# A two-layer graph network on 12,500 nodes and 200,000 edges: the vector path's first part turned behind the second map, edge sources spread by DMA, three result tables in place of four, and h stored by SyncE

## The reference, cut to what matters

```python
# layer 1: attention
h = (x @ W).reshape(N, H, C)
e = leaky_relu(a_src[src] + a_dst[dst]); alpha = softmax of e over dst
out = elu(segment_sum(h[src] * alpha, dst) + bias + x @ skip_W)
x = layernorm(x + out)
# layer 2: equivariant
w = silu(silu(edge_attr @ fc_w1) @ fc_w2) @ fc_w3      # wA, wB, wC, wD per edge
es, ev = ys[dst], yv[dst]                              # mapped node features
m0a = wA * es * sh0
m0b = wD * einsum('eud,ed->eu', ev, sh1) * INV_SQRT3
m1a = wB[:, :, None] * es[:, :, None] * sh1[:, None, :]   # vector path, first part
m1b = wC[:, :, None] * ev * sh0[:, :, None]               # vector path, second part
ns = segment_sum(concat([m0a, m0b]), src)
nv = segment_sum(concat([m1a, m1b]), src)
os_ = ns * dn @ w2_s + sc_s;  ov = nv * dn mapped by w2_v + sc_v   # the second map
x = layernorm(x + normalised concat([os_, ov]))
```

## Time and profile before

| | |
|---|---|
| median of 3 runs | 7266.64 us (7259.7 to 7271.49) |
| profiled execution, its time | 7338.37 us |
| profiled execution, its span | 7335.8 us |
| granted clock of PE, mean | 0.96 |
| busy in the span | PE 88%, DVE 71%, POOL 65%, ACT 57% |
| DMA | 1244.70 MB, mean 170 GB/s |

### The profile page before, as it was taken

One profiled execution on the slowest core, in us unless ns is written; L12 is line 12 of the kernel. 1 busy time (PEld: TensorE's weight loads), 2 busy tenths in 40 slices (PEclk: granted clock), 3 DMA queues, 4 the chain that ended last, 5 costly groups with the idle time before them and its releaser, 6 DMA issues.

```text
span 7335.8 us, 210965 instructions
## 1 busy us (share of the span) xinstructions
PE 6443.9 (88%) x42774; PEld 4394.0 (60%) x42775; DVE 5231.9 (71%) x16784; ACT 4207.1 (57%) x11999; POOL 4802.6 (65%) x4057
## 2 busy tenths in 40 slices
PE   6778777777777777787999999999999999999976
PEld 5444444444444444454777777777777777777754
DVE  3666666667666666799777777777777777777779
ACT  2444444444444444444677777777777777777732
POOL 3555555555555555454677777777777777777778
PEclk8998999999999999888999999999999999999999
DMA  5677777777777777644788888888888888888899
GB/s 181 184 194 197 197 194 193 196 195 197 196 199 193 196 197 196 184 155 147 134 141 140 141 139 141 139 141 139 141 140 140 140 140 141 139 141 139 141 238 300
DMA packets 1213481, 1244.70 MB, mean 170 GB/s; under 512 B 216576, under 2 KB 1124737, under 8 KB 1213345
## 3 DMA queue, kind: packets, MB, share of 16 engines
q0 software_dynamic: 328176, 468.28, 39.5%
q1 hardware_dynamic: 885266, 776.00, 36.4%
HBM read 641.49 MB, written 602.17 MB: 170 GB/s over the span
## 4 chain that ended last, share of the span: by engine, by line
PE 54%; issue 18%; SPq 17%; POOL 4%; DVE 3%; another core or an unknown queue 2%; DMA 1%; ACT 1%; DVEq 1%; POOLq 0%; ACTq 0%
PE PS L929 12%; PE PS L957 12%; PE PS L939 10%; PE PS L976 8%; SPq L398 7%; PE PS L984 5%; SPq L409 2%; PE PS L852 2%; SPq L405 2%; SPq L401 2%; SPq L395 2%; PE PS L989 2%; POOL arena L558 1%; PE PS L842 1%
## 5 line engine op out<-in xcount | busy, mean ns | idle before, releaser
L577 POOL DMA_INDIRECT part<-arena,c_idx x1664 | 2658.4, 1598 | 911.2 <-issue 522.3
L538 POOL DMA_INDIRECT big<-h_tab,big x1664 | 1647.3, 990 | 1217.1 <-PE PS L852 598.0
L852 PE MATMUL PS<-big 128*128 128x260 f32 x3328 | 1092.2, 439 | 387.3 <-DVE big L1172 257.1
L1172 DVE TENSOR_TENSOR big<-big,PS 128x260 f32 x1664 | 701.8, 422 | 684.7 <-PE PS L852 429.8
L1310 DVE TENSOR_TENSOR arena<-PS,arena 128x384 f32<-128x384 f32 x832 | 463.9, 558 | 987.2 <-PE PS L976 958.3
L852 PEld LDWEIGHTS PS<-big 128*128 128x128 f32 x3328 | 580.6, 203 | 760.9 <-issue 653.7
L929 PEld LDWEIGHTS PS<-ident,arena 128*128 128x128 f32 x6656 | 714.4, 141 | 500.3 <-issue 497.7
L929 PE MATMUL PS<-ident,arena 128*128 128x128 f32 x6656 | 909.6, 280 | 2.0 <-DVE arena L1333 2.0
L957 PE MATMUL PS<-arena,w2m 128*64 128x128 f32 (+1 forms) x6656 | 903.3, 392 | 0.0
L722 ACT COPY arena<-PS 128x512 f32<-128x512 f32 x1664 | 894.2, 589 | 10.8 <-PE PS L929 10.4
L939 PE MATMUL PS<-arena 128*128 128x256 f32 x3328 | 856.5, 380 | 1.1 <-ACT arena L744 1.1
(11 more groups left out here) (182 smaller groups left out, 11029.3 us busy)
## 6 DMA issues: line engine op xcount, KB each, us to landing
w_tab<-big SPq DMA_DIRECT2D x416, 520.0 KB
arena<-w_tab SPq DMA_DIRECT2D x1664, 130.0 KB
part<-arena SPq DMA_DIRECT2D x1664, 32.1 KB
ot_tab<-big SPq DMA_DIRECT2D x416, 128.0 KB
arena<-ot_tab SPq DMA_DIRECT2D x416, 128.0 KB
arena<-part SPq DMA_DIRECT2D x392, 128.5 KB, 3.5
big<-h_tab,big POOLq DMA_INDIRECT x1664
part<-arena,c_idx POOLq DMA_INDIRECT x1664
```

Of the source, the lines that this page charges most:

```text
L538: pool.indirect_dma_start(hg[:, s, k, :], None, h_tab, bass.IndirectOffsetOnAxis(ap=sidx[:, s, k:k + 1], axis=0)).then_inc(s_hg[s], 16)
L577: pool.indirect_dma_start(part[q], bass.IndirectOffsetOnAxis(ap=c_idx[:, s, k:k + 1], axis=0), o_cmb[:, s, k, :], None, compute_op=ALU.add ...
L852: mm(PS[:, 2 + k % 2, 0:HW], oh[:, p, k, :], hg[:, p, k, :], start=True, stop=True).then_inc(s_agg, 1)
L1172: v.tensor_tensor(x, x, PS[:, 2 + k % 2, 0:HW], ALU.add).then_inc(s_acc, 1)
```

## The change

Five edits come together.

1. The vector path's first part is wB * es * sh1 for three directions, and the second map does not act on directions. The kernel after puts wB * es alone into `mid` (component 2), maps it once (A), and multiplies the mapped result by `sh1` behind the map (`turned`, DVE), adding the mapped second part (D0, D1, D2). So `mid` has 6 components in place of 8, and 3 transposes of 128 by 128 a tile in place of 4. The map is now S (all 128 rows of the array), A (rows 0 to 63), D0 and D1 together (rows 64 to 127) and D2 (rows 0 to 63), for each of 2 tiles. Five blocks of 128 by 128 are transposed back instead of four. ACT's last copy takes 128 columns (S) where it took 512, and ACT copies `sh1` aside (`c_sh`).
2. The sources of 4 tiles are spread to 128 partitions by one DMA (`same` itself is its target), and DVE compares in place; the load of `c_parts`, the matmul with ones and the bf16 parts in the setup go.
3. Three result tables (`TABLES_OUT`) in place of four: 3 zero stores a step in stage A, 3 loads and 3 matmuls a block in stage D. Add i waits for add i-3. POOL's loop is unrolled by 12.
4. The stores of h go from POOL's program to SP's, between the loads of x and of the weights.
5. On PE the y matmuls of stage C stand ahead of the sum and the count.

The diff, cut to its core:

```diff
-    src_tab = dram("src_tab", [T, 2, P], BF16)
+    src_tab = dram("src_tab", [T, P], F32)
...
-    part = [dram(f"part{k}", [NG * 32 * ZERO, OR], F32) for k in range(GROUP)]
+    part = [dram(f"part{k}", [NG * 32 * ZERO, OR], F32) for k in range(TABLES_OUT)]
...
-        mid = cut(2 * PAIR * 2 * D).rearrange("p (s k c u) -> p s k c u", s=2, k=PAIR, c=8)
-        midT = cut(PAIR * 4 * P).rearrange("p (k c e) -> p k c e", k=PAIR, c=4)
-        oT_sb = cut(4 * P).rearrange("p (j e) -> p j e", j=4)
...
+        mid = cut(2 * PAIR * 6 * MUL).rearrange("p (s k c u) -> p s k c u", s=2, k=PAIR, c=6)
+        midT = cut(PAIR * 3 * P).rearrange("p (k c e) -> p k c e", k=PAIR, c=3)
+        oT_sb = cut(5 * P).rearrange("p (j e) -> p j e", j=5)
...
-        Y_BANK, T_BANK, SR_BANK, OT_BANK, SUM_BANK, CNT_BANK = (0, 1), (2, 3), 4, 5, 6, 7
-        counts = PS[:, CNT_BANK, 0:PAIR * 2].rearrange("p (k c) -> p k c", k=PAIR)
+        c_sh = sb("c_sh", [P, TURN, PAIR, 3])
+        Y_BANK, T_BANK, O_BANK, OT_BANK, SUM_BANK = (0, 1), (2, 3), 4, (5, 6), 7
+        oT = PS[:, 5:7, :].rearrange("p b n -> p (b n)")[:, P:6 * P].rearrange("p (j e) -> p j e", j=5)
+        OT_S, OT_A, OT_D = 0, 1, (3, 2, 4)
+        o_s = PS[:, T_BANK[1], 3 * P:4 * P]
+        o_v = PS[:, O_BANK, :].rearrange("p (j k u) -> p k j u", j=4, k=PAIR)
...
+            load_x(2, 0, CHUNK)
+            store_h(0, 0)
...
+            load(w2m[0:MUL, 2, :], w2_v[MUL:2 * MUL, :])
             for i in range(2):
+                load_x(3 + i, 1 - i, (2 + i) * CHUNK)
+                store_h(1 + i, 1 - i)
...
-                    for k in range(GROUP):
+                    for k in range(TABLES_OUT):
                         sp.dma_start(part[k][ds(g * (32 * ZERO), 32 * ZERO), :].rearrange("(p r) d -> p (r d)", p=32),
                                      zeros[:, :]).then_inc(s_zero, 16)
                     wait(sp, s_wev, 6 * (g - 3))
...
-                if s % 2 == 0 and there(u + 2):
-                    q = (s + 2) % TURN
-                    wait(sp, s_csr, u)
-                    sp.dma_start(c_parts[:, q // 2, :].rearrange("w (k e) -> w k e", k=GROUP),
-                                 src_tab[ds((u + 2) * PAIR, GROUP), :, :].rearrange("k w e -> w k e")
-                                 ).then_inc(s_cpa[q], 16)
...
+                if s % 2 == 0 and there(u):
+                    wait(sp, s_csum, u - 2)
+                    wait(sp, s_ccnt, u - 2)
+                    sp.dma_start(same[:, s:s + 2, :, :].rearrange("p s k e -> p (s k e)"),
+                                 src_tab[ds(u * PAIR, GROUP), :].rearrange("(o k) e -> o (k e)", o=1
+                                                                          ).to_broadcast([P, GROUP * P])
+                                 ).then_inc(s_cpa[s // 2], 16)
...
-            def store_h(c, s):
-                wait_apart(pool, s_hev, 2 * CHUNK * (c + 1))
-                pool.dma_start(hv[ds(c, 1)].rearrange("o p k d -> (o p) k d"), h_out[:, s, :, :]
-                               ).then_inc(s_hst[s], 16)
...
                         wait_apart(pool, s_ccmb, u + 1)
-                        wait_apart(pool, s_add[q], 8 * u - 8 * (s % 2))
-                        pool.indirect_dma_start(part[q], bass.IndirectOffsetOnAxis(ap=c_idx[:, s, k:k + 1], axis=0),
+                        wait_apart(pool, s_add[other], 8 * u + 4 * (k + 4 - TABLES_OUT - other))
+                        pool.indirect_dma_start(part[(r * PAIR + k) % TABLES_OUT],
+                                                bass.IndirectOffsetOnAxis(ap=c_idx[:, s, k:k + 1], axis=0),
                                                 o_cmb[:, s, k, :], None, compute_op=ALU.add).then_inc(s_add[q], 16)
...
+                    a.copy(oT_sb[:, :, :], oT).then_inc(s_coTsb, 1)
...
-                    a.copy(o_sb[:, :, :].rearrange("p k (j u) -> p k j u", j=4),
-                           PS[:, T_BANK[0], :].rearrange("p (j k u) -> p k j u", j=4, k=PAIR)).then_inc(s_cosb, 1)
+                    a.copy(o_sb[:, :, 0:MUL], o_s.rearrange("p (k u) -> p k u", k=PAIR)).then_inc(s_cos, 1)
+                if there(u):
+                    wait(act, s_cw[s], landed(u, s, PAIR))
+                    wait(act, s_cov, u - 3)
+                    a.copy(c_sh[:, s, :, :], wt[:, s, :, D + 1:D + 4]).then_inc(s_csh, 1)
...
-                    for first, n_comps in ((0, 1), (1, 3)):
...
+                    for row, which, chunk, n_chunks, to in ((0, 0, 0, 1, OT_S), (0, 1, 1, 1, OT_A), (MUL, 1, 1, 2, OT_D[0]),
+                                                            (0, 2, 2, 1, OT_D[1])):
+                        rows_used = slice(row, P if which == 0 else row + MUL)
                         for k in range(PAIR):
-                            if first == 0:
+                            if which == 0:
                                 wait(pe, s_cmT, PAIR * (u - 1))
-                            last = mm(PS[k * MUL:(k + 1) * MUL, OT_BANK, first * P:(first + n_comps) * P],
-                                      w2m[:, min(first, 1), :],
-                                      midT[:, k, first:first + n_comps, :].rearrange("p c e -> p (c e)"),
-                                      start=True, stop=True, tile_position=(0, k * MUL))
+                            last = mm(oT[k * MUL:(k + 1) * MUL, to:to + n_chunks, :].rearrange("p j e -> p (j e)"),
+                                      w2m[rows_used, which, :],
+                                      midT[rows_used, k, chunk:chunk + n_chunks, :].rearrange("p c e -> p (c e)"),
+                                      start=True, stop=True, tile_position=(row, k * MUL))
                     last.then_inc(s_coT, 1)
                 if there(u + 1):
...
-                if there(u - 3):
-                    sum_equal()
-                    count()
...
+                    wait(pe, s_coTsb, u - 1 if there(u - 2) else u - 2)
...
                     wait(pe, s_coTsb, u - 1)
-                    wait(pe, s_cmT, PAIR * (u - 1) + 1 if there(u - 1) else PAIR * (u - 1))
-                    for j in range(4):
-                        last = nc.tensor.transpose(PS[:, T_BANK[0], j * P:(j + 1) * P], oT_sb[:, j, :], ident[:, :])
+                    wait(pe, s_cmT, PAIR * u if there(u - 1) else PAIR * (u - 1))
+                    nc.tensor.transpose(o_s, oT_sb[:, OT_S, :], ident[:, :])
+                    wait(pe, s_cov, u - 2)
+                    for j, of in enumerate((OT_A,) + OT_D):
+                        last = nc.tensor.transpose(PS[:, O_BANK, j * P:(j + 1) * P], oT_sb[:, of, :], ident[:, :])
                     last.then_inc(s_co, 1)
-                if m % 2 == 0 and there(u - 1):
-                    wait(pe, s_cpa[m], landed(u - 1, m))
-                    wait(pe, s_csame, u - 1)
-                    mm(PS[:, SR_BANK, :], ones_b, c_parts[:, m // 2, :], start=True, stop=True).then_inc(s_csr, 2)
...
+                    v.tensor_tensor(mid[:, s % 2, :, 3:6, :], y[:, :, 1:4, :], spread(w[:, :, 0, 1, :]), ALU.mult)
...
-                    v.tensor_tensor(mid[:, s % 2, :, 2:8:2, :], spread(q), sh1, ALU.mult)
-                    v.tensor_tensor(mid[:, s % 2, :, 3:8:2, :], y[:, :, 1:4, :], spread(w[:, :, 0, 1, :]), ALU.mult)
+                if there(u - 3):
+                    wait(dve, s_co, u - 2)
+                    wait(dve, s_csh, u - 2)
+                    wait(dve, s_csum, u - 3)
+                    v.tensor_tensor(turned[:, :, :, :], o_v[:, :, 0:1, :].to_broadcast([P, PAIR, 3, MUL]),
+                                    c_sh[:, (s - 3) % TURN, :, :].rearrange("p k (d o) -> p k d o", o=1
+                                                                            ).to_broadcast([P, PAIR, 3, MUL]),
+                                    ALU.mult).then_inc(s_cturn, 1)
...
+                    wait(dve, s_cturn, u - 2)
+                    v.tensor_tensor(o_sb[:, :, MUL:D].rearrange("p k (d u) -> p k d u", d=3), turned[:, :, :, :],
+                                    o_v[:, :, 1:4, :], ALU.add).then_inc(s_cov, 1)
...
-                    v.tensor_tensor(same[:, p:p + 2, :, :].rearrange("p s k e -> p (s k) e"),
-                                    PS[:, SR_BANK, :].rearrange("p (k e) -> p k e", k=GROUP),
-                                    srcF[:, ds((u - 2) * PAIR, GROUP)].rearrange("p (k o) -> p k o", o=1
-                                                                                 ).to_broadcast([P, GROUP, P]),
+                    wait(dve, s_cpa[p // 2], landed(u - 2, p))
+                    eq = same[:, p:p + 2, :, :].rearrange("p s k e -> p (s k) e")
+                    v.tensor_tensor(eq, eq, srcF[:, ds((u - 2) * PAIR, GROUP)].rearrange("p (k o) -> p k o", o=1
+                                                                                         ).to_broadcast([P, GROUP, P]),
                                     ALU.is_equal).then_inc(s_csame, 2)
```

125 lines of the change are left out of this document (65 added, 60 removed).

## The result

The kernel after takes 7142.62 us (7127.75 to 7156.69, 4 runs), the kernel before 7266.34 us (7259.7 to 7271.49, 4 runs) on the same chip. The ratio is 0.9833, 95% interval 0.9813 to 0.9853: 124 us faster, where 567 were forecast. The profiled execution took 7133.53 us.

A forecast was written before the change was run, and what follows sets the result against it. PE was taken to bound stage C and SyncE's queue to pace stage A. Savings of 295 + 250 + 15 + 10 = 570 us from 7266.64 gave 6697, called 6700 us; range 6590 to 7000.

The forecast's parts named there:

- Stage A, 250 us: 165 to 3050 us: one of SyncE's 8 DMAs a step goes, 0.60 us a step, 250 us over 416 steps.
- rival 2: Stage A is not paced by SyncE's zero stores: saves 40 us in place of 250, 6907 us in all; 26%.
- Stage C, PE: 3482 to 7025 us: PE sets the pace; its step falls from 4.255 to 3.78 us.
- the map: Second map on PE in stage C: row halves run side by side, 6 passes for 8, 0.21 us less a step.
- rival 1: The map's row halves don't run side by side: PE's step 4.22 us, stage C saves 29 us, 6963 in all; 12%.
- the wait for D2's weights: In stage C's map, by the skill, D2's weights wait for A: about 0.1 us saved where 0.21 was taken.
- the meshing: Stage C: PE, DVE and POOL at 3.63 to 3.80 us lose some overlap; step 3.90, saving 295 us over 832 steps.
- rival 3: Stage C: DVE, POOL and loads mesh worse; step 4.15 us, 87 us saved in place of 295, 6905 in all; 10%.
- rival 4: Stage C: adds wait for the third before; step 2/3 of landing and wake-up, 3.1 us hidden; slower from 4.58; 4%.
- DVE's sum: Stage C: PE waiting on DVE's sum was named as one way the prediction would be wrong by most.
- Setup: Before stage A: SyncE stores h during POOL's memset, removing PE's 16.87 us stop; 15 us saved, ends 5 and 17.
- Stage D: Behind stage C, 311 us: one of four loads a block goes; 10 us taken, 43 if DMA sets the pace.

The follow-up runs named there:

- e12: The kernel before, unchanged, run on chip 4 for a trace: 6612.94 us.
- e5: The kernel after, unchanged, run again on chip 3: 6518.45 us against 6605.2 for the kernel before, ratio 0.9868.
- e2: The kernel before with one zero store of 128 rows a step in place of four of 32: 7287.71 us against 7326.32, ratio 0.9946.
- e7: The kernel after with four result tables and sources spread as 16-bit integers: 6363.02 us against 6605.2 for the kernel before, ratio 0.9634.
- e11: The kernel after with four result tables and the 16-bit spread, again, on chip 4: 6368.45 us against 6604.5 for the kernel before, ratio 0.9639.
- e8: The kernel after with A, D0, D1 and D2 of the map on all 128 rows, half the weights zero: 6591.9 us, one run.
- e9: The kernel after with four result tables in place of three, on chip 4: 6379.49 us against 6604.5 for the kernel before, ratio 0.9657.
- e10: The kernel after with sources kept and spread as 16-bit integers, on chip 4: 6409.46 us against 6604.5 for the kernel before, ratio 0.9704.

## Why the prediction was wrong

**Stage A, 250 us: the step that failed.** I took the zero store's price from the chain, (0.200 + 0.168) x 6.94 / 4, and the row that spoke against it (SyncE idle for 3 us at 214.93) for a mere discount to 0.60. On chips 3 and 4 a store is worth nothing: 2136.8 us with four (e12), 2137.5 with three (e5). Where stage A was longer, it was worth little: some 8 us on chip 1 by the timed runs, and on chip 2 three stores fewer gave 20 us by the profiled executions and some 28 by the timed ones (e2), while runs of three and four lie 15 us apart. The 89 us between the profiled executions of chip 1 can't be taken as the change's: stage A of the unchanged kernel took 2858 us in one execution and 2838 in another. This was rival 2 (26%): the pace was set elsewhere. The step that failed is the one from "SyncE holds 42% of the chain" to "a store fewer shortens the step", and the chain itself came from a trace with a third of the events that e12's has. What sets the pace of the longer stage A stays open; it comes with the chip or the execution, since the same kernels took 2137 us elsewhere.

**Stage C, PE: a term mis-sized.** A full step of the kernel after, without a wait, against the earlier trace rows:

```profile
5016.92 1.03 PE L977 MATMUL PS<-arena,w2m 128*64 128x128 f32 x16
5017.88 0.87 PE L945 MATMUL PS<-ident,arena 128*128 128x128 f32 x6
5018.59 0.82 PE L993 MATMUL PS<-big,arena 128*128 x6
5019.25 1.04 PE L956 MATMUL PS<-arena 128*128 128x256 f32 x4
...
5020.23 0.31 PE L1004 MATMUL PS<-ident,arena 128*128 128x128 f32 x1
...
5020.91 1.03 PE L977 MATMUL PS<-arena,w2m 128*64 128x128 f32 x16
```

By starts: the map 0.96 us (before 1.01), transposes 0.71 (0.93), y 0.66 (0.66), sum and count 0.98 (0.97), transposes back 0.68 (0.53), and L989's 0.155 is gone: 3.99 for this step, where 3.78 was forecast. Over the whole stage one step in twenty takes 3.97 us or less, in both runs of the kernel after, and where PE never waits (e7, e11) the mean is 3.99. I take 3.97 as PE's own. The transposes came as forecast (-0.22 for -0.23), those back cost 0.15 for 0.12. The map gave 0.05 for 0.21. The starts of its instructions show why; this is one map, each line the start in the trace and the time since the pass before it:

```
us          since   what
5008.699            S, first pass (second column half 0.007 later)
5008.859    0.160   S, second pass
5009.069    0.210   A, first pass (D0 and D1 begin 0.013 later)
5009.229    0.160   A, second pass
5009.338    0.109   D2, first pass
5009.447    0.109   D2, second pass
5009.662    0.215   first transpose of mid
```

A pass behind one of the same shape starts 0.109 later. Where the shape of the array part changes (all rows to half rows, half rows to transposes) the next start comes some 0.1 later, and the second pass after a change comes 0.05 late. The kernel before has such a change on either side of the map; the kernel after has one more in its middle, 0.15 of the 0.21 us. With it gone (e8) the delay in the middle is gone too. D0 and D1 do run beside A: rival 1 (12%) was wrong, and e8 prices it at 0.28. The Trainium skill (TensorE: Matmul & The Clock Gate, Part 3: Packing small matmuls) says that matmuls in different row groups run concurrently, and the trace agrees, with D0 and D1 starting 13 ns behind A. D2 uses the same rows as A, and its first pass starts 0.109 us behind A's second, so the wait for D2's weights that the prediction set beside its sum did not come. What the map fell short by is the change of shape.

**Stage C, the meshing: the other term.** Stage C gained 0.104 us a step for 0.355 (87 us for 295). PE's own step is 0.19 of what is missing, and the meshing 0.06: I took 0.12 us for it (3.78 to 3.90), and it was 0.18 above PE's own 3.97 on chip 1, 4.149. That the result is rival 3's step (4.15, 10%) is luck, since rival 3 stood on a PE step of 3.78. Its reason was right in one part, the spreading load that delays adds; DVE's chain was not the trouble. The mechanism is rival 4's, the wait for the third add, and it was mis-sized in both of its terms. For the landing I had 3.9 us from a store in another stage, and for the wake-up 0.73. From the packet records of the trace I worked out when each add's last closing packet ended, after the start of its instruction (a closing packet is one of the 16 small ones that end an add; taken in order of issue, 1100 adds of stage C):

```
                         median   90%    95%   (us)
before (chip 1)            3.89   4.23   4.28
after (chip 1)             4.38   5.25   5.43
after, four tables (e9)    4.41   5.36   5.49
after, 16 bits (e10)       4.27   5.07   5.24
after, both (e11)          4.29   4.98   5.16
```

So the 3.9 us fitted the kernel before by luck, and the kernel after has 0.5 us more in the middle and over 1 us more in the tail. The spreading load is what was added to the traffic there; with it and four tables the landings are as late. The wake-up was too small as well: in some 420 cases where POOL stood idle for the add three back (chip 1), the next add started 1.11 us (median) after that landing, and none of all 1664 started sooner than 1.01 us after it. By the prediction's own formula, 2/3 of landing and wake-up, the median gives 3.66 us a step and the 95% landing 4.36, against PE's 3.97: estimates, but they say that the middle is hidden and the tail is not. POOL can catch up little, as two adds take 3.71 us of a step (1.549 and 0.305 each). With four tables four adds fit between, and the same landings cost nothing: in e9 every add started at least 1.76 us after the fourth before it had landed, so none was held by it. What such a loss looks like, in the timeline of the kernel after (start, duration, in brackets idle time and what ended it):

```profile
5002.33 1.55 POOL L588 DMA_INDIRECT part<-arena,c_idx  x1 [0.30 <-issue]
...
5004.99 0.59 ACT L752 COPY arena<-PS 128x512 f32<-128x512 f32 x1 [2.60 <-DMA part<-arena,c_idx]
...
5005.47 0.20 ACT L753 COPY arena<-c_num 128x2 f32<-128x2 f32 x1
5005.57 0.27 ACT L757 COPY arena<-PS 128x128 f32<-128x128 f32 x1
5005.67 1.77 POOL L588 DMA_INDIRECT part<-arena,c_idx  x1 [1.79 <-ACT arena L753]
...
5005.98 0.52 PE L945 MATMUL PS<-ident,arena 128*128 128x128 f32 x3 [1.83 <-ACT arena L757]
```

One add, started at 4998.62, landed only at 5004.38, 5.76 us later. It was the third before POOL's next one, which started at 5005.67. The profile puts POOL's 1.79 us down to ACT's L753, but ACT had written that add's slot at 4995.57 already. With POOL behind, all four slots of `o_cmb` were full. ACT waited 2.60 us to write the next one (L752, for the landing of the same add), its copy of S (L757) queued behind it, and PE waited 1.83 us for that. This chain, from ACT's slot wait to PE, is what I had not named: I had named DVE's sum. DVE was not the trouble: it is busy 1670 us in 2000, 3.46 a step, where I had 3.63.

**The rest.** Setup: 13 us for the 15 forecast, by the mechanism forecast. The matmuls (L809) that stood still for 16.87 us now wait 1.67 and 0.53, since SyncE stores the first chunk at 54.78, during POOL's memset:

```profile
50.87 10.43 POOL L527 MEMSET big<- 128x12370 f32 x1
...
53.00 4.73 PE L809 MATMUL PS<-big 128*128 128x264 f32 x20 [1.67 <-issue]
...
54.78 0.40 SPq L367 DMA_DIRECT2D h_tab<-big  x1
...
58.26 6.50 PE L809 MATMUL PS<-big 128*128 128x264 f32 x28 [0.53 <-ACT big L627]
```

Stage D: 3 us for 10. One load in four went and it hardly mattered, so its DMA share of 0.92 was no bound. Stage B was left at nothing and gained 7 to 13 us, at the ends that the marks put into it. The sum with the measured terms where stage A is short (e12 less e5): 16 + 0 + 7 + 69 + 1 = 93 us, beside the 87 of the timed runs (6605.2 - 6518.45).

## What to carry to other kernels

A chain that runs through a queue shows where time is spent, not that the queue is the bound. If the queue stands idle for part of each step while the step keeps its length, something else sets the pace; test it with a run that takes work off the queue before pricing anything there. Count the semaphore events of a trace against those of another run of the same kernel before believing its chain and its waits. When a buffer count falls (four tables to three) beside more traffic, price the wait with the landing's tail under the new traffic and not with its middle under the old, and take the wake-up from a row where an engine really waited for a landing. Splitting the array into row halves pays only if the saved passes outweigh a further change of shape, about 0.15 us here.
